# GpSimd's scaling of the raw weight slices: a tensor times a column given as a scalar, or a product of two tensors

## The reference

```
x = x + _L0_xattn_ref(_layernorm(x), ctx_4096, ...)
x = x + _L0_ffn_ref(_layernorm(x), L0_ffn_W, ...)
x = x + _L1_xattn_ref(_layernorm(x), ctx_4096, ctx_4096, mask, wq, wk, wv, wo, 0)
x = x + _L1_ffn_ref(_layernorm(x), L1_ffn_W_up, ...)
...
q = (query @ wq).reshape(bs, sq, N_Q_HEADS, D_K).transpose((0, 2, 1, 3))
...
attn = jax.nn.softmax(masked, axis=-1)
out = jnp.einsum('bhqk,bhkd->bhqd', attn, v)
...
return out @ wo
```

## Time and profile before

| | |
|---|---|
| Median of 3 runs | 2034.71 us (2030.98 to 2035.88) |
| The profiled execution | 2036.05 us |
| Its span from the first to the last instruction | 2034.3 us |
| Matrix engine PE busy | 1976.0 us |
| VectorE DVE busy | 1605.2 us |
| ScalarE ACT busy | 1105.9 us |
| GpSimd POOL busy | 1247.3 us |

### The profile page before, as it was taken

The page is one execution under the profiler, slowest core; times in us unless marked ns, Lnnn a source line. Parts: engine busy times, 40 slices in busy tenths (PEclk is TensorE's granted clock), DMA queues, the critical chain, the costliest instruction groups (busy, mean ns, idle before and its releaser), DMA issues.

```text
span 2034.3 us, 26140 instructions
## 1 busy us (share of the span) xinstructions
PE 1976.0 (97%) x9140; PEld 1114.2 (55%) x9140; DVE 1605.2 (79%) x2705; ACT 1105.9 (54%) x1722; POOL 1247.3 (61%) x751
## 2 busy tenths in 40 slices
PE   8999999999989999999999999999999999999899
PEld 6876786878634444444444444444444444444587
DVE  5877697576788888888888889888888888878643
ACT  5553534436466666566656656566566665666300
POOL 1542353422167787787788877788887788785500
PEclk9999999999999999999999999999999999999899
DMA  7662546547898787887778899987787887887612
GB/s 261 197 213 94 172 144 205 177 140 232 266 222 165 157 171 148 177 166 166 161 157 169 168 221 203 213 168 163 159 167 168 160 178 144 174 150 155 185 64 72
DMA packets 673379, 349.54 MB, mean 172 GB/s; under 512 B 576768, under 2 KB 601600, under 8 KB 673248
## 3 DMA queue, kind: packets, MB, share of 16 engines
q1 hardware_dynamic: 673248, 347.87, 71.8%
HBM read 173.73 MB, written 31.46 MB: 101 GB/s over the span
## 4 chain that ended last, share of the span: by engine, by line
PE 78%; DVE 7%; issue 2%; DMA 2%; ACT 1%; POOL 1%; SPq 1%; ACTq 0%; DVEq 0%; POOLq 0%
PE ps L43 25%; PE ps L44 25%; PE ps L45 25%; PE ps L914 1%; DMA pT<-pp 1%; POOL u_sb L2246 1%; DVE pp L1748 1%; DVE psb L1733 1%; DVE t_sb L1293 1%; DVE t_sb L1295 1%; PE ps L921 0%; SPq L688 0%; DVE vhl_sb L1389 0%; DVE u_sb L1292 0%; PE ps L1175 0%
## 5 line engine op out<-in xcount | busy, mean ns | idle before, releaser
L1748 DVE SCALAR_TENSOR_TENSOR pp<-psb,st,pp 128x1024 f16<-128x1024 f32 x256 | 403.8, 1577 | 2.6 <-ACT pp L2139 0.5
L2132 ACT ACTIVATE psb<-psb,st 128x1024 f32<-128x1024 f32 x256 | 294.1, 1149 | 174.1 <-DVE st L1733 173.9
L1733 DVE CUSTOM_DVE_ANT_0 psb<-ps,mask,sc 128x1024 f32<-128x1024 f32 x256 | 328.0, 1281 | 71.4 <-PE ps L45 71.2
L2139 ACT ACTIVATE pp<-psb,st 128x1024 f16<-128x1024 f32 x256 | 293.5, 1146 | 162.0 <-DVE st L1743 159.2
L2289 POOL TENSOR_SCALAR araw<-araw,kst 128x512 f32<-128x512 f32 x128 | 316.3, 2471 | 46.6 <-DMA araw<-in_wq 46.6
L2289 POOL TENSOR_SCALAR araw<-araw,sc 128x512 f32<-128x512 f32 x128 | 243.4, 1902 | 0.5 <-DMA araw<-in_wo 0.5
L2295 POOL TENSOR_TENSOR wol<-araw,woh 128x512 f16<-128x512 f32 x128 | 149.3, 1167 | 117.0 <-ACT woh L2071 117.0
L1764 DVE SCALAR_TENSOR_TENSOR x_lo<-ps,sc,x_lo 128x512 f32<-128x512 f32 x256 | 190.8, 746 | 25.4 <-PE ps L45 25.3
L43 PE MATMUL ps<-woh,osb 128*128 128x512 f16 x512 | 194.6, 380 | 10.3 <-issue 6.0
L43 PE MATMUL ps<-ksb,qsb 128*128 128x512 f16 x512 | 194.3, 380 | 5.3 <-DVE st L1733 5.3
L43 PE MATMUL ps<-pT,vsb 128*128 128x512 f16 x512 | 194.4, 380 | 4.6 <-DMA pT<-pp 4.6
(11 more groups left out here) (303 smaller groups left out, 3902.3 us busy)
## 6 DMA issues: line engine op xcount, KB each, us to landing
araw<-in_wq SPq DMA_DIRECT2D x128, 256.0 KB, 4.4
araw<-in_wo SPq DMA_DIRECT2D x128, 256.0 KB, 4.4
scan<-in_wq SPq DMA_DIRECT2D x64, 256.0 KB, 4.5
scan<-in_wo SPq DMA_DIRECT2D x64, 256.0 KB, 4.7
raw<-in_wv SPq DMA_DIRECT2D x16, 512.0 KB, 4.6
raw<-in_ctxT SPq DMA_DIRECT2D x16, 512.0 KB, 4.2
raw<-in_wk SPq DMA_DIRECT2D x16, 512.0 KB, 5.3
raw<-in_ctx SPq DMA_DIRECT2D x16, 512.0 KB, 4.5
```

Of the source, the lines that this page charges most:

```text
L1733: e.tensor_tensor_reduce(out=psb[:, n % 3, :], in0=pair(n % 2 * 2), in1=mask[:, i, :], scale=sc[:, 23 - H // 32:24 - H // 32], scalar=-LOW ...
L1748: e.scalar_tensor_tensor(out=pp[:, r, 1024:2048], in0=psb[:, r, :], scalar=st[:, n // 4 % 4, 16 + i:17 + i], in1=pp[:, r, 0:1024], op0=ALU ...
L2132: e.activation(P, P, ACT.Exp, bias=c[:, i:i + 1], scale=-1.0, accum_out=c[:, 8 + i:9 + i]).then_inc(a_exp.sem, 1)
L2139: e.activation(pp[:, r, 0:1024], psb[:, r, :], ACT.Copy, scale=st[:, n // 4 % 4, 16 + i:17 + i]).then_inc(a_ph.sem, 1)
```

## The change

The scaling on POOL is given as another operation with the same result: in place of `tensor_scalar`, which takes the 128x1 column as a scalar of each partition, `tensor_tensor`, which takes it as a second tensor of 128x512 whose 512 elements in a partition are all at the same address. Input, output, the place in POOL's program and all semaphores are as they were, for all 256 slices. No instruction of any engine is added, taken away or moved.

```
@@ -2286,7 +2286,7 @@
                     e.wait_ge(v_ws.sem, v_ws["v", 8])
                 G = W_ORDER[n][1] // 8 % 8
                 scale = sc[:, 17:18] if wo else kst[:, 30 + G:31 + G]
-                e.tensor_scalar(w_raw(n), w_raw(n), scale, None, ALU.mult).then_inc(p_ws.sem, 1)
+                e.tensor_tensor(w_raw(n), w_raw(n), scale.broadcast_to([128, 512]), ALU.mult).then_inc(p_ws.sem, 1)
 
         def split_w(key):
```

## The result

The changed kernel takes 2045.68 us, the median of 4 runs (2043.94 to 2047.1), beside 2034.07 us (2030.98 to 2035.88, 4 runs) of the kernel before on the same chip. The ratio is 1.0057, with a 95% interval of 1.0042 to 1.0072: slower, by more than the 0.3% that I took as the bound. The profiled execution has a span of 2043.8 us, 9.5 more than before.

The account below looks back on a forecast made before the run. The prediction took PE to bound the kernel. It added 0.6 us at the start of the attention and 1.8 in struck heads, 2.4 in all, to the median of 2034.71, giving 2037.1, with a range of 2027 to 2048.

Parts of the forecast that it names:

- likeliest case: Whole kernel: 2.4 us slower, 2037.1, counted as no change; chance 0.57 together with the rival that nothing moves.
- first rival: Attention heads: hold strikes all 20 late-`o_lo` heads, 7.4 us, plus 6 through `o_lo`; 2048.7, chance 0.20.
- slack of 0.5: Fourth tile's `p_lo` before `values`: DVE delays up to 0.5 us cost nothing, beyond that PE pays one for one.
- The price of the new scaling: Scaling on POOL: 1.26 us bare, low end 1.16, high end 2.35, against 1.56 for the old form.
- The hold: POOL's scaling shutting out `p_lo` on DVE: 0.58 us longer than the old form's 0.48.
- A duration that is off by 0.04 decides it, and I take a quarter of them: 5 x 0.37 = 1.8 us: Second scaling against `p_lo` where DVE had won: a quarter of 20 heads make PE wait 0.37 each.
- faster rival: `ua` addition on POOL wins its race in odd heads, `o_lo` in time: up to 6.4 us, 2028.3; chance 0.17.
- inside the slack of 0.5. Cost: 0: Heads where POOL had won: the fourth tile's `p_lo` is held off for 0.3 us, costing PE nothing.
- Against it: a struck head makes PE wait, which gives DVE time: Argument against the hold striking all 20 heads: PE's wait also moves the next head out of step.
- The start of the attention, 0.6 us: First tiles of the attention, where DVE is the chain: the scaling at 585.25 holds `p_lo`, 0.6 us.
- DVE's busy time, up by some 10 us: Sign expected in the changed profile: DVE busy some 10 us more.
- about 30 x 2/3 = 20: Heads asking for a new `o_lo`: POOL's addition loses its race in two of three, so 20 pay 0.32 us.

Follow-up runs that it names:

- e4: Kernel before, with only the 128 slices of wo scaled by the new product and those of wq as before: 2038.90 us, ratio 1.0010.
- e5: The changed kernel run again with no edit: 2045.64 us, ratio 1.0068 to the kernel before.
- e1: The changed kernel with five short writes of a 128x1 column behind each new scaling on POOL: 2042.02 us, ratio 1.0022 to the kernel before.
- e11: The changed kernel with 17 short writes of a 128x1 column behind each scaling of slices 8 to 251: 2040.09 us, ratio 1.0021 to the kernel before.
- e2: The kernel before with the old scaling on only 320 of 512 columns, the other 192 left unscaled: 2032.92 us, ratio 0.9986.

## Why the prediction was right and where it was wrong

The range held the time: 2045.68 lies between 2027 and 2048. The likeliest case, no change at 2037.1, didn't happen. The time is near that of the first rival, "the hold strikes", at 2048.7, to which I gave 0.20, and the signs that I had named for it are there: heads of 21.4, and a mean of line 1748 above 1.7. Its sum is right partly by luck. The 7.4 us that it puts on the odd heads for the fourth tile are 0 there, and the even heads, which it leaves free, pay 6.5.

- **Who bounds the kernel and where the loss would show:** right. PE is the bound, all of the loss is in the 59 heads, and what lengthens them are the two things that I had named, `o_lo` and the fourth tile's `p_lo`. Which heads pay for which I had wrong (below). The slack of 0.5 is shown by the 4.55 of the struck head.
- **The price of the new scaling:** mis-sized. "I take 1.26, for the same types; the low end is 1.16"; it measured 1.04, outside my bounds. POOL's busy time fell by 177 us and not by 60 to 80. The bare saving is 256 x 0.52 = 133; the rest is that POOL waits less behind `p_lo`, since it gets in first more often: scalings of 0.3 or more above the bare time fell from 162 to 118 of 256.
- **The hold:** I took 1.06 from the f32 form, so 0.58 longer than the 0.48 of the old one; it measured 0.83, 0.35 longer. The sign held, and it is what makes a quicker instruction a slower kernel.
- **The step that failed, "A duration that is off by 0.04 decides it, and I take a quarter of them: 5 x 0.37 = 1.8 us".** I had put the point at which POOL gets in first at 1.30 us and taken 1.26. At 1.04 the second scaling comes 0.3 ahead of `p_lo` (1115.74 and 1116.04), so in 19 of the 26 odd heads it isn't a race at all. But the price was wrong too: the fourth tile's `p_lo` ends 4.70 or more ahead of `values` in each of the 26, and PE's way from the product with wo to `values` is the 12.95 of before. I had that margin shrink from 5.08 by 0.87, beyond the slack of 0.5; it shrank by 0.38, to 4.70. The term of 5 x 0.37 = 1.8 us measured 0. e4 shows the same with the loss of the even heads mostly gone.
- **The odd heads' real loss:** 0.3 us in 16 heads, by `o_lo`, as the wake of the struck even head in front. The rival had the place ("if the 0.3 that `p_lo` falls behind in the other heads also reaches `o_lo`", 6 us), but the likeliest case left it out. It measured 26 x 0.13 = 3.4 us, since four more heads than before won the addition's race and gained 0.3 each; that is a part of the faster rival.
- **The even heads, "inside the slack of 0.5. Cost: 0":** wrong. I moved each row by 0.3 and saw one hold of 0.3. What the trace shows is a subtraction with the next scaling behind it without a gap, so that `p_lo` is held over the end of the one and 0.84 of the other, 0.86 in all. 27 even heads went from a mean of 20.72 to 20.96, 0.24 each. This is the greater part: 27 x 0.24 = 6.5 us against 26 x 0.13 = 3.4 for the odd ones (in e5 7.0 and 5.5). e1 and e11, in which POOL is later by 0.15 and 0.55, take nearly all of this part away: 20.74.
- **"Against it: a struck head makes PE wait, which gives DVE time":** it helps little, if at all; only five of 27 even heads stayed at 20.7. Whether the seven odd heads at 20.72 owe their won race to it is not shown.
- **The start of the attention, 0.6 us:** the first of the five `values` came 2 us earlier, not later. That start lies between 620.7 and 627.5 in the profiles of the experiments, so a term of 0.6 can't be seen there.
- **DVE's busy time, up by some 10 us:** 30. The hold strikes more rows than those that cost PE anything.
- **The count of heads with a late `o_lo`, "about 30 x 2/3 = 20":** the share of two in three is a mean over both kinds. In the kernel before, 23 of the 26 regular odd heads lose the race and 15 of the 27 even ones. And 59 x 0.21 is 12.4, not 12.6.

The Trainium skill (SBUF — State Buffer, SBUF: two separate sides) has the shared port as held for a whole instruction. The measured holds, 0.48 of 1.56 and 0.83 of 1.04, differ from it; by it the old form would be the worse one, and e2, with the old form at 1.08 us and no loss, goes against that. The skill (GPSIMD Engine Reference, Performance versus the Vector engine) puts a floor of about 2.6 cycles for an element on operations with two inputs; by it the new form would be the slower one, and here the old takes 1.56 and the new 1.04. The estimate that the prediction took from it, 1.11 for the new form, is near; its 0.44 for the old one isn't.

## What to carry to other kernels

An operation on GpSimd has two prices, the time that it takes and the time for which it keeps a two-input operation of VectorE out. An instruction that is a third shorter may have the dearer of the second kind, and then only the second reaches the bound. Where the path has a slack of tenths of a microsecond, don't shift single rows on paper. Look for two instructions that can come to stand back to back ahead of the one on the path, follow a delay into the next head, and see what stands in the queue ahead of an operation that PE waits for. The order on DVE, not the scaling, was worth 0.3 to 0.4% here.

## What I had not expected of the hardware

- A product with a column that is read for every element takes 1.04 us at 128x512 f32; with a full f32 row it takes 1.26, and by a scalar for each partition 1.56.
- The operations of GpSimd let a two-input operation of VectorE go at different times: 0.48 of 1.56 (by a scalar; 0.32 of 1.08 with 320 columns), 0.83 of 1.04 (by a column), 0.96 of 1.16 and 1.06 of 1.26 (by a full row).
- Writes of a 128x1 column on GpSimd follow each other at 0.03 to 0.04 us (17 in 0.63), though the trace gives each 0.09 by itself.
- One half of the change costs 0.1%, the other too, and both together 0.6%.
